# A causal mask moved from VectorE to TensorE in the last attention of a nine-block network, and two filler products fewer in three routers

## The reference

```python
# attention 3 (the one with a causal mask): 12 heads of 16 channels
scores = jnp.einsum('bhqd,bhkd->bhqk', q, k) * (1.0 / math.sqrt(D))
causal = jnp.tril(jnp.ones((T, T), dtype=bool))
scores = jnp.where(causal, scores, -jnp.inf)
att = jax.nn.softmax(scores, axis=-1)
y = jnp.einsum('bhqk,bhkd->bhqd', att, v)
x = x + y.transpose(0, 2, 1, 3).reshape(B, T, C) @ c_proj_w.T
# the experts: every token takes two of eight, by the largest router logits;
# its position among the tokens of that expert gives its slot
top_vals, top_idx = jax.lax.top_k(logits, TOP_K)
pos = jnp.cumsum(onehot, axis=0) - onehot
```

## Time and profile before

| | us |
|---|---|
| median of three runs | 401.25 |
| lowest, highest run | 400.78, 403.18 |
| profiled execution, its device time | 403.34 |
| span of the profiled execution (first to last instruction) | 401.5 |
| TensorE busy in the span | 376.3 (94%) |
| VectorE busy | 247.5 (62%) |
| ScalarE busy | 175.0 (44%) |
| GpSimd busy | 108.8 (27%) |

### The profile page before, as it was taken

The page is one execution under the profiler, slowest core; times in us unless marked ns, Lnnn a source line. Parts: engine busy times, 40 slices in busy tenths (PEclk is TensorE's granted clock), DMA queues, the critical chain, the costliest instruction groups (busy, mean ns, idle before and its releaser), DMA issues.

```text
span 401.5 us, 9820 instructions
## 1 busy us (share of the span) xinstructions
PE 376.3 (94%) x3806; PEld 248.0 (62%) x3806; DVE 247.5 (62%) x662; ACT 175.0 (44%) x441; POOL 108.8 (27%) x166
## 2 busy tenths in 40 slices
PE   8999999999999999999999988989999999999996
PEld 6776645566777645666676755746666655655444
DVE  3776488765476587764576587442246577547773
ACT  1488234441278253540397178322143445243351
POOL 5821356310001365310001301320024442026330
PEclk9999899999999999999999999899999999999999
DMA  6399940071399700091499500327990301991000
GB/s 189 80 308 300 365 91 2 2 203 36 115 244 381 221 2 3 2 212 27 147 231 336 191 1 2 118 61 252 312 307 18 91 2 53 284 309 66 2 2 20
DMA packets 28680, 56.09 MB, mean 140 GB/s; under 512 B 5260, under 2 KB 15963, under 8 KB 28635
## 3 DMA queue, kind: packets, MB, share of 16 engines
q1 hardware_dynamic: 26978, 53.88, 45.8%
q10 hardware_dynamic: 1657, 1.60, 1.2%
HBM read 53.25 MB, written 2.22 MB: 138 GB/s over the span
## 4 chain that ended last, share of the span: by engine, by line
PE 68%; DVE 11%; issue 9%; ACT 6%; DVEq 2%; DMA 1%; POOL 1%; SPq 1%; POOLq 0%; ACTq 0%
PE bank L1419 11%; PE bank L1351 8%; PE bank L1358 5%; PE bank L1009 5%; PE bank L1378 4%; ACT sw L821 4%; PE bank L1135 4%; PE bank L1162 3%; PE bank L1447 3%; PE bank L1048 3%; PE bank L1178 2%; PE bank L1434 2%; PE bank L1144 2%; PE bank L1253 2%; PE bank L1286 2%
## 5 line engine op out<-in xcount | busy, mean ns | idle before, releaser
L821 ACT ACTIVATE sw<-bank,nmax 128x256 f32<-128x256 f32 (+1 forms) x96 | 43.3, 478 | 11.7 <-DVE nmax L1650 7.4
L906 ACT ACTIVATE hT<-bank 128x384 f32<-128x384 f32 x34 | 16.4, 489 | 67.5 <-PE bank L1378 67.5
L1009 PE MATMUL bank<-warm 128*128 128x256 f32 x158 | 44.5, 424 | 1.2 <-DVE warm L1951 1.2
L1836 DVE COPY sw<-rw 128x1344 f32 (+1 forms) x32 | 31.2, 985 | 9.7 <-PE bank L1366 6.0
L646 POOL COPY sw<-rinv 128x64 f32<-128x64 f32 x48 | 9.7, 238 | 96.2 <-DVE rinv L1663 93.0
L1009 PEld LDWEIGHTS bank<-warm 128*128 128x128 f32 x158 | 31.7, 212 | 5.5 <-DVE warm L1951 1.2
L1419 PE MATMUL bank<-sw,hT 128*32 128x192 f32 x630 | 32.6, 330 | 0.0
L710 POOL COPY sw<-rw 128x1344 f32 (+1 forms) x12 | 21.7, 1812 | 37.5 <-PE bank L1366 24.2
L1135 PE MATMUL bank<-kT,qT 64*128 64x256 f32 (+1 forms) x192 | 24.1, 380 | 4.2 <-ACT sw L821 3.0
L1162 PE MATMUL bank<-consts,sw 128*128 128x128 f32 x180 | 25.5, 279 | 2.4 <-issue 1.1
L1419 PE MATMUL bank<-rw,hT 128*32 128x192 f32 (+1 forms) x432 | 25.9, 330 | 1.4 <-ACT hT L906 1.4
(11 more groups left out here) (234 smaller groups left out, 739.9 us busy)
## 6 DMA issues: line engine op xcount, KB each, us to landing
rw<-in_M_w_dram SPq DMA_DIRECT2D x16, 1152.0 KB, 16.3
rw<-in_M_w_dram SPq DMA_DIRECT2D x16, 768.0 KB, 7.0
rw<-in_M_w_dram SPq DMA_DIRECT2D x36, 192.0 KB, 8.0
rw<-in_M_w_dram SPq DMA_DIRECT2D x8, 576.0 KB, 9.1
wqkv<-in_A_wqkv_dram SPq DMA_DIRECT2D x4, 432.0 KB, 4.1
rw<-in_M_w_dram SPq DMA_DIRECT2D x16, 96.0 KB, 5.1
wproj<-in_A_wproj_dram SPq DMA_DIRECT2D x4, 288.0 KB, 5.0
bqkv<-in_A_bqkv_dram SPq DMA_DIRECT2D x3, 288.0 KB, 4.5
```

Source lines behind the costliest of these rows:

```text
L821: act.activation(probs[:, p % 2, h, t, 0:keys_of(n, t)], scores_bank(p, h)[:, t, 0:keys_of(n, t)], ACT.Exp, bias=nmax[:, p % 2, h, t:t + 1 ...
L1009: pe.matmul(bank[b][:, 0:T], warm[:, 0:P], warm[:, :], start=True, stop=True)
L1836: dve.tensor_copy(sw1[:, 1 + i, 0:n1], rw1[:, bass.ds(ids[4 * i + d], 1), 0:n1].rearrange("p a n -> p (a n)")).then_inc(w1c_dve, 1)
```

## The change

In attention 3 VectorE no longer adds the mask. TensorE adds it instead: behind each score product follows a second one, identity (16 bits, `counting[:, 2]`) times the mask in 16 bits (`later_keys`), accumulated onto the 128 x 128 square of the diagonal. That is four more products per pair of heads, 24 in all, each over 128 rows, 128 columns of weights and 128 columns of data; they stand one by one between the score products of the two heads. GpSimd makes `later_keys` with one more cast at the start, ahead of the three others, and TensorE waits for four casts instead of three. `WARM_ROUTER` goes from 4 to 2: two fillers fewer ahead of the positions of experts 0, 1 and 2.

```diff
-WARM_LN, WARM_ROUTER = 3, 4
+WARM_LN, WARM_ROUTER = 3, 2
...
+        later_keys = sb("later_keys", [P, P], BF16)
...
+            pool.tensor_copy(later_keys[:, :], consts[:, CONST["causal"]]).then_inc(counting_ready, 1)
             pool.tensor_copy(counting[:, 0], consts[:, CONST["earlier"]]).then_inc(counting_ready, 1)
...
                     for t in range(TT):
                         for h in range(2):
                             ins = pe.matmul(scores_bank(p, h)[:, t, 0:keys_of(n, t)], qT[head_rows(h), p, t * P:(t + 1) * P],
-                                            kT[head_rows(h), p, 0:keys_of(n, t)], start=True, stop=True)
+                                            kT[head_rows(h), p, 0:keys_of(n, t)], start=True, stop=n < 3, skip_group_check=n == 3)
+                            if n == 3:
+
+                                ins = pe.matmul(scores_bank(p, h)[:, t, t * P:(t + 1) * P], counting[:, 2], later_keys[:, :],
+                                                start=False, stop=True, skip_group_check=True)
                             if t == TT - 1:
                                 ins.then_inc(s_psum, 1)
...
-                    pe.wait_ge(counting_ready, 3)
+                    pe.wait_ge(counting_ready, 4)
...
                         if n == 3:
-
-                            mask = consts[:, CONST["causal"]].unsqueeze(1).broadcast_to([P, TT, P])
-                            own_keys = bank[B_S[p % 2][h]][:, 0:TT * (T - P) + TT * P].rearrange("p (a k) -> p a k", k=P)[:, 0:4:3]
-                            then(dve.tensor_tensor(own_keys, own_keys, mask, ALU.add))
-                            settle()
                             for t in range(TT):
```

## The result

The changed kernel takes 414.12 us in the median of four runs (410.97 to 415.36), the kernel before 401.19 in the same round of runs: ratio 1.0283, 95% interval 1.0238 to 1.0328. The prediction said slower, 407.1 us, and at most 410.0; the direction came true, the size did not. The profiled execution took 414.37 us, its span is 412.6.

The account below looks back on a forecast made before the run. No engine was full; the last chain lay 68% on PE and 11% on DVE, whose masks sat on it in attention 3. Profiled 403.34 us + 6.5 (attention 3) - 2.7 (routers) = 407.1 us; range 402.5 to 410.

Parts of the forecast that it names:

- Part 1: Attention 3: twelve mask sums of 0.42 us and the waits behind them leave DVE; at most 2.6 us of the chain.
- Part 2: Attention 3: 24 more PE products; tile changes make a pair 2.72 us against 0.65; stage +6.5 us, bounds -2.6 to +8.7.
- Rival D: Masks empty the array twice each, and with fillers cut the clock falls late in all three routers: 410.5 us, chance 0.08.
- Part 3: Routers: two fillers fewer give -1.4 in experts 0 (0.2 goes back), 0 in experts 1, -1.5 in experts 2; sum -2.7 us.
- the 0.2 put down for dispatch products: Experts 0: about 0.2 us of the 1.4 gained goes back, as earlier dispatch products meet the rest of the low clock.
- its -1.5: Experts 2: with two fillers fewer the positions start near 260.05 instead of 261.54, so -1.5 us.
- the range of -2.9 to +3.6: Routers: ends of the fillers' effect in us; likelier, late clock falls could cost up to 1.2 a block.
- Part 4: Start, POOL: one more cast of 0.29 us moves what follows by at most that; 0, or 0.29 if cover were gone.

Follow-up runs that it names:

- mask alone: Against the kernel before: attention 3's mask on TensorE in the change's order, four fillers kept; 410.48 us, ratio 1.0198; once more on a second chip 410.97 us, 1.0191.
- change again: The whole change (interleaved masks on TensorE, two fillers) run once more on a second chip, against the kernel before: 413.50 us, ratio 1.028.
- fillers alone: Against the kernel before: `WARM_ROUTER` 4 to 2 and nothing else, mask sums still on DVE; 402.62 us, ratio 1.0009.
- grouped: Against the changed kernel: a pair's four score products first, then its four masks, one start per bank; four fillers 399.63 us (0.9940), two fillers 401.14 us (0.9960).
- 32-bit masks: Against the changed kernel: same interleaved order, mask as a 32-bit product instead of 16 bits, four fillers; 414.38 us, ratio 1.0294.

## Why the prediction was wrong in size

**Part 1** was right: no mask on DVE, and what it was worth in the stage, 2.9 us by the kernel without masks, lies just above the 2.6 that the chain showed.

**Part 2** was right in its mechanism and its prices: a pair of 2.73 us where 2.72 was summed, PE without a wait, 28.2 us of stage worked out for the full clock. It failed at the step that was never written down, that the stage keeps the clock of 1.00 which rows 2 show for the kernel before. The new order has one head's half of the array at work at a time, with a gap at each change, and the clock fell for 6.8 us once (mask alone, change again), twice (the changed kernel) or longer. The term was +6.5, and its upper end +8.7; it measured +12.2 = 6.4 + two falls of 2.9. Rival D had the clock fall, but in the routers only; the prediction had the reason at hand, since it found the low clock in rows 7 behind work that used the array thinly, and did not ask it of the order it had just worked out.

**Part 3** failed by its sum. The -2.7 took the fall of the clock as something the fillers suffered, so that fewer of them would suffer less. In the profiled execution experts 0 gave -0.44, experts 1 +1.10 and experts 2 -1.74, together -1.1; over many runs the edit alone gives nothing measurable. The step that failed is the 0.2 put down for dispatch products that "meet the rest of the low clock": the low stretch comes later and lies over the dispatch and the products behind it. Experts 1's +1.10, where 0 was forecast, goes with a fall that the mask alone, with four fillers, has there too. That experts 2 came so near its -1.5 is luck: the clock did not fall there in that execution at all, and the mask alone, with no fall there either, needs 146.2 us from its residual sum to the end (262.5 to 408.7), against 146.1. Of the range of -2.9 to +3.6 the upper side, for likelier falls, had the direction. Outside attention 3 (and but for the last microsecond) the profiled executions with two fillers have 10.2 to 13.7 us at the low clock (the change 13.7, again 10.2, fillers alone 13.7, grouped 13.7); the eight with four fillers have 3.4 or 6.8. One execution of each is a small count, and two of these stretches lie in experts 3 and 4, where no filler was cut; but the runs' mean clocks go the same way (median 0.987 with two fillers alone, 0.995 before), and so the four fillers seem to earn in clock what they cost in time.

**Part 4** held: the time to attention 0's residual sum differs by 0.1. The forecast of 407.1 thus lay 7.3 under the profiled 414.37: 5.7 by attention 3, 1.6 by the routers.

Whether the two parts add up is settled only in part. Mask and fillers together cost 3.6 us more than the mask alone in the first runs, which were not of one round (414.12 and 410.48), and 2.5 on one chip (413.50 and 410.97, where the mask alone spreads over 10 us); the fillers alone cost 0.5, with grouped masks 1.5. Of the profiled executions, the change again and the first of the mask alone have the same stage (31.07 and 31.08), and the change loses 3.0 in the rest of the span, with low stretches in experts 1, 2 and 4 where the other has one in experts 1. Whether fewer fillers also make falls in attention 3 likelier was not shown.

## What to carry to other kernels

Price a product added to TensorE by its neighbours, not by its columns: products in different rows of the array run side by side for nothing until one over all rows comes between them, and each change of shape then cost 0.09 us here, and on the way back a bare weight load of 0.11; put such products together, as the grouped masks did (with four fillers ratio 0.994, where the interleaved ones gave 1.020). And where an edit leaves TensorE busy in name but thinly used, work out the time at the low clock level as well, and don't count fillers ahead of it as pure cost.

## What the runs showed of the hardware that was not expected

TensorE's clock fell to 1.2 GHz while the timeline shows the engine without any wait: from the stage's start at 232.5 to the fall at 236.1 it had done only score products over 64 rows and 16-bit masks. The Trainium skill, page "TensorE: Matmul & The Clock Gate", section "A second HAM failure mode: psum-queue depth-cycling", reports that short idle times between groups of products can make the clock swing; the rows here agree in kind, as PE is recorded busy for 6.80 of 6.80 us at the low clock, and the only gaps ahead of it are the 0.09 us at each change of shape; but the 32-bit masks kept 1.00 with the same gaps and more work between them, so short gaps alone did not do it here. The low stretches were not of one length: 3.4 us in most routers, 6.8 in some routers and in attention 3, 13.7 in one run.
